# Attention in a fused transformer stack: products with values four key blocks at a time, and score products over 96 or 98 contraction rows

## What is computed

```python
def attention(x):                       # per batch, 1024 tokens, head size 32
    q, k, v = heads(x @ Wq), heads(x @ Wk), heads(x @ Wv)   # a0: biases and rotary factors as well
    att = einsum('bhqd,bhkd->bhqk', q, k) / sqrt(32)
    att = where(causal, att, -inf)
    att = softmax(att, axis=-1)
    y = einsum('bhqk,bhkd->bhqd', att, v)
    return merge(y) @ Wo
```

## Time and profile before

| | |
|---|---|
| median of 3 runs | 2869.77 us (2869.21 to 2873.86) |
| the profiled execution | 2869.56 us |
| its span | 2867.8 us |
| TensorE busy | 2674.4 us (93%), 13216 matmuls |
| VectorE busy | 1336.4 us (47%) |
| ScalarE busy | 1094.3 us (38%) |
| GpSimd busy | 637.4 us (22%) |
| mean granted TensorE clock | 0.98 of 2.4 GHz |

### The profile page before, as it was taken

One profiled execution on the slowest core, in us unless ns is written; L12 is line 12 of the kernel. 1 busy time (PEld: TensorE's weight loads), 2 busy tenths in 40 slices (PEclk: granted clock), 3 DMA queues, 4 the chain that ended last, 5 costly groups with the idle time before them and its releaser, 6 DMA issues.

```text
span 2867.8 us, 35771 instructions
## 1 busy us (share of the span) xinstructions
PE 2674.4 (93%) x13216; PEld 2017.0 (70%) x13216; DVE 1336.4 (47%) x2712; ACT 1094.3 (38%) x1994; POOL 637.4 (22%) x1105
## 2 busy tenths in 40 slices
PE   5889879998999999999999998999999899999999
PEld 4677755566556788778888877664766477888887
DVE  5776555545554434443333335554455453333333
ACT  6545325554565322332212222556355642221211
POOL 2332432232222322521111111113211331111110
PEclk8999989999999999999999999999999999999999
DMA  3211021102121010000000002223222200000001
GB/s 136 66 58 64 15 67 43 35 31 61 39 61 49 1 62 12 16 30 23 22 30 26 23 19 60 53 54 83 52 54 57 72 23 23 22 30 26 23 19 59
DMA packets 60654, 121.63 MB, mean 42 GB/s; under 512 B 11840, under 2 KB 12864, under 8 KB 60480
## 3 DMA queue, kind: packets, MB, share of 16 engines
q1 hardware_dynamic: 60480, 119.35, 14.9%
HBM read 63.73 MB, written 13.63 MB: 27 GB/s over the span
## 4 chain that ended last, share of the span: by engine, by line
PE 77%; DVE 8%; issue 5%; ACT 4%; DMA 2%; SPq 2%; POOL 1%; DVEq 0%; ACTq 0%; POOLq 0%
PE psum L746 59%; PE psum L866 7%; PE psum L831 5%; PE psum L848 3%; PE psum L755 1%; SPq L1427 1%; ACT tmp L919 1%; DVE s1a0masked L1233 1%; ACT s4a1e L1045 1%; DVE s4a1masked L1233 1%; PE psum L886 1%; POOL x L1341 0%; DVE tmp L1205 0%; DVE s0f0prod L1139 0%; PE psum L838 0%
## 5 line engine op out<-in xcount | busy, mean ns | idle before, releaser
L746 PE MATMUL psum<-hA_hi,wmem 128*128 128x256 f32 (+1 forms) x1536 | 408.5, 339 | 23.2 <-DVE s0f0dso L1167 6.4
L746 PEld LDWEIGHTS psum<-hA_hi,wmem 128*128 128x128 f32 x1536 | 271.7, 193 | 63.0 <-DVE s1a0negmax L1233 8.5
L746 PE MATMUL psum<-hA_lo,wmem 128*128 128x512 f32 (+1 forms) x864 | 297.1, 344 | 0.0
L1233 DVE CUSTOM_DVE_ANT_0 s4a1masked<-psum,mask_q 128x640 bf16<-128x640 f32 (+7 forms) x256 | 188.6, 755 | 142.0 <-PE psum L831 89.8
L1233 DVE CUSTOM_DVE_ANT_0 s1a0masked<-psum,mask_q 128x640 bf16<-128x640 f32 (+7 forms) x256 | 188.2, 755 | 125.6 <-PE psum L831 73.6
L1045 ACT ACTIVATE s1a0e<-psum,p_scale 128x384 f32<-128x384 f32 (+5 forms) x384 | 203.6, 589 | 110.4 <-PE psum L848 108.1
L1045 ACT ACTIVATE s4a1e<-psum,p_scale 128x384 f32<-128x384 f32 (+5 forms) x384 | 203.9, 588 | 91.0 <-PE psum L848 89.7
L1172 DVE SCALAR_TENSOR_TENSOR x<-psum,x 128x512 f32<-128x512 f32 x256 | 176.4, 689 | 101.1 <-PE psum L746 96.4
L1143 DVE TENSOR_TENSOR s3f1prod<-psum,s3f1silu 128x512 f32<-128x512 f32 x64 | 44.3, 692 | 305.2 <-PE psum L746 302.4
L746 PE MATMUL psum<-s3f1w,s3f1a 128*128 128x512 f32 x768 | 186.0, 397 | 0.0
L1143 DVE TENSOR_TENSOR s5f1prod<-psum,s5f1silu 128x512 f32<-128x512 f32 x64 | 44.3, 692 | 304.0 <-PE psum L746 301.1
(11 more groups left out here) (208 smaller groups left out, 5054.8 us busy)
## 6 DMA issues: line engine op xcount, KB each, us to landing
s1a0qst<-s1a0qs SPq DMA_DIRECT2D x96, 128.0 KB
s4a1qst<-s4a1qs SPq DMA_DIRECT2D x96, 128.0 KB
s4a1kst<-s4a1ks SPq DMA_DIRECT2D x96, 128.0 KB, 2.3
raw<-in_gate SPq DMA_DIRECT2D x44, 256.0 KB, 2.7
raw<-in_up SPq DMA_DIRECT2D x44, 256.0 KB, 2.7
raw<-in_down SPq DMA_DIRECT2D x44, 256.0 KB, 2.7
rounded<-s0f0w SPq DMA_DIRECT2D x24, 256.0 KB, 2.0
s2f0w<-rounded SPq DMA_DIRECT2D x24, 256.0 KB, 4.9
```

Source lines behind the costliest of these rows:

```text
L746: ins = pe.matmul(out_, w, m, start=n == 0, stop=n == len(terms) - 1)
L1233: dve.tensor_tensor_reduce(T[s]["masked"][b][turn % 2][:, 0:width].rearrange("p (z w) -> p z w", **bare), scores, mask_q[:, SEQ - width:SE ...
```

## The change

`pv` becomes due when six blocks stand in the list (`PV_BLOCKS` + `PV_LAG`), and then the four oldest go: blocks 0 to 3 behind unit 5, blocks 4 to 7 behind unit 1 of the next head. `row` contracts over 96 rows (`STACK`) and `key` over 98. The clears, their semaphores and waits, and the fourth DMA of each q stack are gone; a new step `k_ones` on GpSimd, at the start of a stage behind `v_ones`, writes the ones in rows 96 and 97 of `kst` for all four places by one memset, and `key` waits for it.

```diff
-PV_LAG = 3
+PV_BLOCKS, PV_LAG = 4, 2
+STACK = 3 * HD
...
         plan.append(("v_ones", s))
+        plan.append(("k_ones", s))
...
-            first, clears = Beside(plan), Beside(plan)
-            if b == 0:
-                clears.waiting += [[[("clear", s, j)]] for j in range(HPG)]
+            first = Beside(plan)
...
-                clears.tick()
             beside_o.flush()
-            clears.flush()
...
-                if len(behind) > PV_LAG and i % 2 == 1:
-                    times_v(*behind.pop(0))
-                    times_v(*behind.pop(0))
+                if len(behind) == PV_BLOCKS + PV_LAG:
+                    for _ in range(PV_BLOCKS):
+                        times_v(*behind.pop(0))
...
-                stack_count[n, j] += 64 if n == "q" else 48
+                stack_count[n, j] += 48
...
-                    ins = pe.matmul(ps[:, z, 0:pw], q_st[:, j, i * P:(i + 1) * P],
-                                    k_st[:, j, z * pw:(z + 1) * pw], start=True, stop=True)
+                    ins = pe.matmul(ps[:, z, 0:pw], q_st[0:STACK, j, i * P:(i + 1) * P],
+                                    k_st[0:STACK, j, z * pw:(z + 1) * pw], start=True, stop=True)
...
-                pe.matmul(ps[:, 0, 0:pw], k_st[:, j, jt * P:(jt + 1) * P],
-                          q_st[:, j, q0 + z * pw:q0 + (z + 1) * pw], start=True,
+                on.wait_ge(sem["k_ones"], at("k_ones", "k_ones", s))
+                pe.matmul(ps[:, 0, 0:pw], k_st[0:STACK + 2, j, jt * P:(jt + 1) * P],
+                          q_st[0:STACK + 2, j, q0 + z * pw:q0 + (z + 1) * pw], start=True,
                           stop=True).then_inc(sem["s_k"], 1)
...
-            def clear(s, j):
-                q_st, k_st = T[s]["qst"], T[s]["kst"]
-                dve.memset(q_st[3 * HD:P, j, :].bitcast(F32), 0.0).then_inc(sem["q_clear"], 1)
-                dve.memset(k_st[3 * HD:P, j, :].bitcast(F32), 0.0).then_inc(sem["k_clear"], 1)
-                on.wait_ge(sem["k_clear"], at("k_clear", "clear", s, j))
-                dve.memset(k_st[3 * HD:3 * HD + 2, j, :].bitcast(F32),
-                           1.0).then_inc(sem["k_put"], 1)
...
+            def k_ones(s):
+                on.wait_ge(sem["v_ones"], at("v_ones", "v_ones", s))
+                pool.memset(T[s]["kst"][STACK:STACK + 2, :, :].bitcast(F32),
+                            1.0).then_inc(sem["k_ones"], 1)
+                on.wait_ge(sem["k_ones"], at("k_ones", "k_ones", s))
...
-                on.wait_ge(sem["q_clear"], at("q_clear", "clear", s, j))
-                on.wait_ge(sem["k_put"], at("k_put", "clear", s, j))
...
-                if n == "q":
-                    sp.dma_start(st[3 * HD:3 * HD + 2, j, :].bitcast(F32),
-                                 t["kst"][P - 2:P, j, :].bitcast(F32)
-                                 ).then_inc(stacked[n][j], 16)
```

More of the change, by code:

```diff
@@ L313 @@
     "gu": ("gate", "up", "silu", "prod", "a_hi"), "a_lo": ("a_lo",),
-    "clear": ("q_clear", "k_clear", "k_put"), "v_ones": ("v_ones",),
+    "k_ones": ("k_ones",), "v_ones": ("v_ones",),
     "piece": ("proj",), "v_tile": ("v_mm",), "v_chunk": ("v_mm", "v_bias"), "v_turn": ("v_tp",),
@@ L1286, in vector_program @@
                      "q8": q8_, "q_b": q_b, "gu": gu, "a_lo": a_lo, "down": down,
-                     "clear": clear, "piece_out": piece_out, "row": row, "m_lo": m_lo,
+                     "piece_out": piece_out, "row": row, "m_lo": m_lo,
                      "y_fin": y_fin, "y_tp": y_tp, "oproj": oproj}
@@ L1363, in gpsimd_program @@
             steps = {"begin": begin, "ln_stats": ln_stats, "w_split": w_split,
-                     "down": down, "v_ones": v_ones, "bias_x": bias_x,
+                     "down": down, "v_ones": v_ones, "k_ones": k_ones, "bias_x": bias_x,
                      "e_mask": e_mask}
@@ L1438, in m_lo @@
                 for p, (name, kind) in enumerate(ready):
-                    dst = t["qst"][3 * HD + p:3 * HD + p + 1, j, :].bitcast(F32)
+                    dst = t["qst"][STACK + p:STACK + p + 1, j, :].bitcast(F32)
                     on.wait_ge(sem[name], at(name, kind, s, b, n))
```

## The result

| | before | after |
|---|---|---|
| median | 2869.49 us (2868.94 to 2873.86, 4 runs) | 2962.89 us (2951.94 to 2971.88, 4 runs) |
| the profiled execution, its span | 2869.56, 2867.8 us | 2971.88, 2970.1 us |
| mean granted TensorE clock, of 2.4 GHz | 0.977 | 0.962 |
| TensorE busy | 2674.4 us | 2712.0 us |

The ratio is 1.0320, 95% interval 1.0283 to 1.0357: 93 us slower, where +46 was forecast, and 16 us beyond the upper end of the range. The direction was right, the size was not. The four executions of the changed kernel lie 20 us apart, and they order by their clock: 2951.94 us at 0.970, 2960.63 at 0.966, 2965.14 at 0.965, 2971.88 at 0.962. The profile is that of the slowest of the four, 9 us above the median.

The account below looks back on a forecast made before the run. TensorE's own sequence was taken as the bound (77% of the last-ending chain). Loops +63 us, stage starts -17, contraction 0: net +46 on 2869.56 us, forecast 2915 us, range 2866 to 2947.

Parts of the forecast that it names:

- What bounds the kernel: TensorE holds 77% of the chain that ended last, so only what lengthens or shortens its own sequence counts.
- stretch A: Units (key blocks) 2 to 5 of a plain head: work beside pv grows from 3.74 to 4.49 us, +0.75 us.
- stretch B: Units (key blocks) 6, 7, 0, 1 across two heads: work other than pv grows from 2.85 to 3.74 us, +0.89 us.
- the plain head: Attention head without projection products, 10.97 us before in stage 1: +1.37 us there, +1.2 us in stage 4.
- the pv groups: Per head, four groups taking 4.38 us become two taking 4.11 us: -0.27 us.
- heads with products: 18 attention heads holding projection products: a 1.4 us product covers what pv covered; +0.2 us each, +3 us.
- +63: Attention loops' total in us: +36 for stage 1's plain heads, +24 for stage 4's, +3 for heads with products.
- The start of the stages: Clears and one stack DMA removed: -11.5 us in stage 1, -4.5 in stage 4, -1 for SP's queue; together -17.
- Contraction over 96 or 98 rows: In row and key, streamed columns stay the same, so 0; -7 us if shorter weight loads were quicker in proportion.
- rival (c): 96-row and 98-row matmuls count as different modes, draining between row and key: at most 152 us, about 3000 us; chance 0.04.
- Rival (a): Other engines keep up with TensorE, so every saved pv switch (0.34 us) counts in full: 2809 us; chance 0.10.
- Rival (b): Only stretch B is laid bare, as ScalarE isn't late in stretch A: 2877 us; chance 0.20.

Follow-up runs that it names:

- e8: Kernel before with only the new pv order, each row's maximum taken over half its columns and the exponent scaled by 0.001: 2892.39 us, ratio 1.0076.
- e1: Kernel before with only the new pv order (groups of four); clears, fourth DMA and 128 contraction rows stay: 2941.88 us, ratio 1.0245.
- e2: Changed kernel with pv put back to pairs behind units 3, 5, 7 and 1: 2856.92 us, ratio 0.9949.
- e11: Same kernel as e2, run again beside e9 and e10 on the same chip: 2859.01 us, ratio 0.9957.
- e10: Kernel before with only the contraction over 96 and 98 rows; pairs, clears and fourth DMA stay: 2873.53 us, ratio 1.0013.
- e5: e1 plus only the contraction over 96 and 98 rows; clears and fourth DMA stay: 2975.32 us, ratio 1.0376.
- e4: Changed kernel with pv of one block at a time, eight groups per head: 2925.18 us, ratio 1.0187.
- e9: Changed kernel with three pv groups per head, of 2, 4 and 2 blocks behind units 3, 7 and 1: 2961.78 us, ratio 1.0321.
- e7: Changed kernel with two extra 128-row matmuls of 512 columns per head ahead of m_tp's wait for VectorE: 2931.19 us, ratio 1.0206.
- e6: Changed kernel with only key back over 128 rows, the unused rows zeroed by GpSimd once a stage: 2948.23 us, ratio 1.0270.

## Why the prediction was wrong in size

- **What bounds the kernel, stretch A, stretch B, the plain head, the pv groups: right.** 12.34 us against 12.34, its three parts each within 0.03 us, and e8 showed by the maxima what the waits were. In stretch A the releaser differs in one detail: row 4 follows m_tp by 0.26 us, so it was m_tp's wait for VectorE that counted, not row 4's for ScalarE. Row 4 was forecast 2.2 us behind row 2 by ScalarE's exponentials, and it came 2.17 us behind (row 2 at 457.81, m_tp at 459.72, row 4 0.26 us later). Another wait ended at about the same time, so that stretch A fits to 0.01 us is partly luck.
- **Plain heads with another pattern:** in the last group of stage 1, and in stage 4, a head goes from 11.44 to 12.42 and from 11.43 to 12.43: +1.0, where I had +1.37 and +1.2. Some 3 to 4 us too much in either stage.
- **The failed term of the sum: heads with products.** "A product of 1.4 us in a stretch covers what pv covered, in stretch B in full" is refuted. Timeline of PE in the changed kernel, stage 1, with four products (L744) around:

```profile
539.79 0.27 PE L836 MATMUL psum<-ident,s1a0negmax 128*8 128x128 f32 x1 [1.73 <-DVE s1a0negmax L1224]
...
547.38 0.67 PE L829 MATMUL psum<-s1a0kst,s1a0qst 96*128 96x448 f32 x2
...
549.44 0.63 PE L829 MATMUL psum<-s1a0kst,s1a0qst 96*128 96x512 f32 x2
...
552.30 0.39 PE L829 MATMUL psum<-s1a0kst,s1a0qst 96*128 96x256 f32 x1 [1.52 <-DVE s1a0negmax L1224]
```

  Timeline of DVE there:

```profile
549.71 0.48 DVE L1196 SCALAR_TENSOR_TENSOR tmp<-psum,s1a0bcol,s1a0ropeq 128x256 f32<-128x256 f32 x1 [0.53 <-PE psum L744]
550.68 0.42 DVE L1200 TENSOR_TENSOR s1a0qs<-tmp,s1a0qs 128x256 fp32r<-128x256 f32 x1 [0.48 <-ACT s1a0qs L997]
551.02 1.22 DVE L1224 CUSTOM_DVE_ANT_0 s1a0masked<-psum,mask_q 128x1024 bf16<-128x1024 f32 x1
```

  The product between rows 6 and 7 pushes row 7 back, from 0.62 us behind row 6 in a plain head to 2.06 here. And it comes with an output step that stands on VectorE ahead of row 7's maximum and waits there for ScalarE: 549.71 to 551.02, 1.31 us, some 0.9 of it after row 7's matmuls ended (549.44 + 0.63). So it covers TensorE and delays VectorE as well: rows 0 and 1 wait 0.48 and 0.29 us in a plain head, row 1 here 1.52, in place of nothing. m_tp waits 1.73 us at the start of this head, 0.59 in a plain one. In e1, whose trace is at the full clock in these heads of stage 4 and nearly all of stage 1, the two m_tp distances that the products of stage 1 fall into are +2.3 us together in a typical case (14.39 to 16.32, 14.45 to 14.81), the three in stage 4 +3.9 (14.77 to 15.81, 15.67 to 17.67, 13.45 to 14.27) in four cases and +2.4 to +2.7 in two, where the forecast had 1.6 for either: 6 x 0.7 + 4 x 2.3 + 2 x 1 = 15 us too little, against the 8 too much above, 7 of the 10 us between +63 and the 72.6 of e1. Most of the rest stands in one later head of each batch of stage 4 (14.98 to 16.73, 13.66 to 16.17), where e1's clock does fall.
- **The start of the stages: right in sign, -17 forecast.** Timeline of DVE in the changed kernel, which answers the earlier trace rows:

```profile
379.45 0.48 DVE L1196 SCALAR_TENSOR_TENSOR tmp<-psum,s1a0bcol,s1a0ropeq 128x256 f32<-128x256 f32 x1 [8.12 <-DMA s1a0bo<-in_bo]
...
384.05 0.47 DVE L1196 SCALAR_TENSOR_TENSOR tmp<-psum,s1a0bcol,s1a0ropeq 128x256 f32<-128x256 f32 x1
```

  The three steps to the fourth output take 4.6 us where 15.4 stood, so 10.8 are gone behind the first one; but the first output itself waits for the DMA of the biases and comes 2.4 us later. The first row is 7.8 us earlier in this execution (402.7 to 394.9), where 11.5 was the term. It moves by some us from run to run: 399.0 to 404.8 in the five traces with clears, 392.1 to 395.4 in the nine without, 8.6 us between the means. Stage 4 gives 3.2 (875.2 to 1778.4, now 934.4 to 1834.4) where 4.5 was. Runs: -14 (e2), -14.5 (e11 against e10).
- **The failed step: "Contraction over 96 or 98 rows. Columns streamed stay the same, so 0", and a sum with no clock in it.** Alone it is near 0 (e10: +2 us). Behind waits laid bare it is +33 us (e5 against e1), through the granted clock, 0.94 and 0.91 in e5's stage 1 and 0.88 and 0.91 in the changed kernel's, where e1 has 0.98 twice. The range had no term from above for this edit, only -7 to 0; the only price above 0 was rival (c)'s. Rival (c) had the right suspect, the row counts, with the wrong mechanism: no drain is seen between row and key, and its place in the trace (matmuls of 256 columns further apart) shows nothing: 453.37 to 453.49 is 0.12 us as before.
- **Rival (a)** is refuted by e1, though its price was about right: e4 has 0.27 us a switch against its 0.34. What two groups fewer gave back was less than the waits that they laid bare. The Trainium skill (TensorEngine Tiling (Array Packing), Key Properties) says that a change of mode drains TensorE. e4's 0.27 us agree with it, but no run parts a drain from the rest of the price. Rival (b) would have the plain head at 11.6; it was 12.34.

By e1 and e2 the forecast would have had to be +71 - 14 = +57; it was +46. The remaining 36 of the 93 us are the pair's, which with the 11 us between +46 and +57 makes up the miss of 48 us, to rounding. What stays open is why fewer contraction rows let the clock fall more often: runs show that it does, by how much, and that filling the wait or shortening it stops most of it; they show nothing of the mechanism. `row` alone back over 128 rows was not tried.

## What to carry to other kernels

A group of matmuls that waits for nobody is cover for the engine that is late; before joining such groups, list for every place that one leaves what that engine has queued there, output steps of other products included. Sum the waits that a change lays bare twice: once for themselves, and once for what they may do to TensorE's clock in the group behind them, above all when the same change makes the matmuls narrower in rows. Test the parts of a change alone and together: here one part gained 14 us, one cost 71, and together they cost 93.

## What the runs showed of the hardware

- In the changed kernel two waits of 0.59 and 0.73 us, 1.2 us apart, were followed by 3.1 us at a granted clock of 0.50 (1.2 GHz) in which TensorE never paused, and in e9 a wait of 1.05 us (0.44 shortly before it) by 3.43 us at 0.59. The first cost its head about 1.6 us (14.06 against 12.4). Behind waits of 0.59 and 0.45 us the clock stayed full in the changed kernel's head at 447.38.
- With the same waits (TensorE idle for 139.4 and 133.0 us in the loops), the time lost to the clock there was about 19 us over 128 rows (e1) and 67 over 96 and 98 (the changed kernel).
- Contraction over 96 and 98 in place of 128 rows, columns unchanged: no time saved in a matmul (row 5's two of 384 columns take 0.46 us to the next start, 449.23 to 449.69 in the changed kernel, and 0.46 in e1), but a lower clock where there are waits: 0.965 (e5) against 0.977 (e1) over the whole run.
- 32 us were gained by two matmuls of no use in every head (e7), and 15 by contracting over rows that are zero (e6).
